# Masked attention: one exponential of 1024 columns over two score banks instead of two of 512

## What is computed

```
scores = jnp.einsum('bgrqd,bgkd->bgrqk', q, k) / jnp.sqrt(jnp.float32(HD))
scores = jnp.where(causal_mask[None, None, None, :, :], -jnp.inf, scores)
scores = jnp.where(padding_mask[:, None, None, None, :], -jnp.inf, scores)
w = jax.nn.softmax(scores, axis=-1)
out = jnp.einsum('bgrqk,bgkd->bgrqd', w, v)
```

## Time and profile before

| | us |
|---|---|
| median of three runs | 1663.35 |
| profiled execution, own time | 1665.44 |
| its span | 1663.5 |
| masked attention, end of its last result on DVE | 554 |
| exponentials of this block (L703), busy | 138.5 |

### The profile page before, as it was taken

One profiled execution on the slowest core, in us unless ns is written; L12 is line 12 of the kernel. 1 busy time (PEld: TensorE's weight loads), 2 busy tenths in 40 slices (PEclk: granted clock), 3 DMA queues, 4 the chain that ended last, 5 costly groups with the idle time before them and its releaser, 6 DMA issues. The chain is left out here.

```text
span 1663.5 us, 22309 instructions
## 1 busy us (share of the span) xinstructions
PE 1410.6 (85%) x8402; PEld 662.6 (40%) x8402; DVE 811.4 (49%) x1326; ACT 722.6 (43%) x1356; POOL 401.5 (24%) x475
## 2 busy tenths in 40 slices
PE   4587786786766688988589999997999999999998
PEld 3254453453432244544212222223444444444443
DVE  6564465465463578775376666652640320320220
ACT  2175556455446277777336556564440220220220
POOL 7111011011002367767322222214540000000000
PEclk9598998898988799999879999998999999999999
DMA  5636535525423201011353434323331001000000
GB/s 151 140 100 167 131 110 160 135 84 145 117 70 108 89 19 33 33 45 50 90 153 111 139 116 138 100 90 114 110 106 64 12 1 45 31 0 25 26 0 26
DMA packets 89283, 140.65 MB, mean 85 GB/s; under 512 B 8264, under 2 KB 47752, under 8 KB 88656
## 3 DMA queue, kind: packets, MB, share of 16 engines
q1 hardware_dynamic: 76384, 114.16, 24.6%
q10 hardware_dynamic: 12800, 25.17, 4.7%
HBM read 105.85 MB, written 33.46 MB: 84 GB/s over the span
## 5 line engine op out<-in xcount | busy, mean ns | idle before, releaser
L1634 DVE TENSOR_REDUCE c_negmax<-c_psA 128x1 f32<-128x512 f32 x256 | 165.7, 682 | 88.9 <-PE c_psA L1699 87.5
L1966 PE MATMUL d_psGU<-d_zt_hi,d_w_hi 128*128 128x512 bf16 x512 | 195.6, 382 | 3.7 <-ACT d_silu L1899 2.3
L830 DVE TENSOR_REDUCE a_negmax<-a_psX 128x4 f32<-128x1024 f32 x128 | 151.0, 1217 | 95.7 <-PE a_psX L1049 95.7
L1966 PE MATMUL d_psGU<-d_zt_lo,d_w_hi 128*128 128x512 bf16 x512 | 195.5, 382 | 0.0
L1966 PE MATMUL d_psGU<-d_zt_hi,d_w_lo 128*128 128x512 bf16 x512 | 195.3, 381 | 0.0
L1899 ACT ACTIVATE d_silu<-d_psGU 128x512 f32<-128x512 f32 x64 | 38.2, 597 | 348.3 <-PE d_psGU L1966 348.3
L1592 ACT ACTIVATE c_probs<-c_psB 128x512 f32<-128x512 f32 x256 | 140.1, 594 | 108.7 <-PE c_psB L1712 108.6
L703 ACT ACTIVATE a_probs<-a_psB 128x512 f32<-128x512 f32 x256 | 138.5, 596 | 98.6 <-PE a_psB L1061 73.7
L1929 DVE TENSOR_TENSOR d_h<-d_psGU,d_silu 128x512 f32<-128x512 f32 x64 | 44.2, 691 | 223.4 <-PE d_psGU L1966 223.1
L1049 PE MATMUL a_psX<-a_ks,a_qs 113*128 113x256 bf16 x512 | 88.6, 312 | 70.4 <-DMA a_qs<-q_scr 46.8
L1061 PE MATMUL a_psB<-a_qs,a_ks 115*128 115x256 bf16 x512 | 94.0, 299 | 40.2 <-ACT a_probs L703 28.6
(11 more groups left out here) (217 smaller groups left out, 2589.9 us busy)
## 6 DMA issues: line engine op xcount, KB each, us to landing
a_tern_stage<-in_w ACTq DMA_DIRECT2D x32, 768.0 KB, 4.7
d_weight_stage<-in_w_last SPq DMA_DIRECT2D x24, 512.0 KB, 3.7
a_ks<-k_scr SPq DMA_DIRECT2D x8, 768.0 KB
a_qs<-q_scr SPq DMA_DIRECT2D x8, 768.0 KB
c_ks<-k_scr SPq DMA_DIRECT2D x48, 128.0 KB, 2.6
c_qs<-q_scr SPq DMA_DIRECT2D x48, 128.0 KB, 3.0
a_xz<-in_x SPq DMA_DIRECT2D x32, 128.0 KB, 7.0
a_ctx<-in_ctx_t SPq DMA_DIRECT2D x8, 512.0 KB, 9.2
```

The costliest lines, as they stand in the source:

```text
L830: v.tensor_reduce(negm[:, u, :], X[:, 2 * (u % 2):2 * (u % 2) + 2, :].rearrange("p a (j k) -> p (a j) k", k=SEQ), AX.X, ALU.max, negate=Tr ...
L1634: v.tensor_reduce(negm[:, u:u + 1], A[:, u % 2, :], AX.X, ALU.max, negate=True)\
L1966: last = pe.matmul(GU[:, 2 * up + i % 2, :], wgu[wh][:, i, up, k, :], zt[zh][:, k, :], start=(k == 0 and j == 0), stop=(k == DC - 1 and j ...
```

## The change

Line numbers in the text are those of the kernel before.

The two exponentials of a pair become one ACTIVATE that reads both banks, 1024 columns, and writes the whole pair of `a_probs`. `score_units` is raised once a pair, by the second unit; `exp_done` once a pair. On PE only the first unit of a pair waits, for the exponential of the pair before it (all of it); the second unit waits for nothing. `weigh` waits for the same exponentials as before, counted in pairs; SyncE's wait at the start of batch 7 is the same point, counted in pairs.

```diff
--- before.py
+++ after.py
@@ -552,7 +552,7 @@
                     stack(b + 2)
                 if b + 1 == BATCH:
 
-                    sp.wait_ge(s["exp_done"], 4 * GROUPS * b)
+                    sp.wait_ge(s["exp_done"], 2 * GROUPS * b)
                     front.sync(sp)
                 for j in range(QJ):
                     sp.wait_ge(s["x_updated"], ST * b + j // (QJ // ST) + 1)
@@ -697,12 +697,10 @@
 
                 g = e // 2
                 need(act, s["pv_done"], GROUPS * b + g - 1)
-                for jj in range(2):
-                    u = 2 * e + jj
-                    act.wait_ge(s["score_units"], 4 * GROUPS * b + u + 1)
-                    act.activation(pr[:, e % 4, :, jj * P:(jj + 1) * P].rearrange("p r (a i) -> p a r i", a=2),
-                                   B[:, u % 2, :].rearrange("p (a r i) -> p a r i", a=2, r=SHARE), ACT.Exp,
-                                   scale=HD ** -0.5).then_inc(s["exp_done"], 1)
+                act.wait_ge(s["score_units"], 2 * GROUPS * b + e + 1)
+                act.activation(pr[:, e % 4].rearrange("p r (a i) -> p a r i", a=QJ),
+                               B[:].rearrange("p j (a r i) -> p (j a) r i", a=2, r=SHARE), ACT.Exp,
+                               scale=HD ** -0.5).then_inc(s["exp_done"], 1)
 
             def attend(b):
                 for g in range(1, GROUPS):
@@ -1052,21 +1050,23 @@
                 last.then_inc(s["max_units"], 1)
 
             def score_unit(b, e, jj):
-                par, grp, kt, u = b % 2, e // 2, e % 2, 2 * e + jj
+                par, grp, kt = b % 2, e // 2, e % 2
                 queries = qflat[par][0:K_ALL, SHARE * grp * SEQ:SHARE * (grp + 1) * SEQ]\
                     .rearrange("p (c j n) -> p c j n", c=2, j=QJ)
-                need(pe, s["exp_done"], 4 * GROUPS * b + u - 1)
+                if jj == 0:
+                    need(pe, s["exp_done"], 2 * GROUPS * b + e)
                 for a in range(2):
                     j = 2 * jj + a
-                    last = pe.matmul(B[:, u % 2, a * SEQ:(a + 1) * SEQ], ks[par][0:K_ALL, j, grp, kt * P:(kt + 1) * P],
+                    last = pe.matmul(B[:, jj, a * SEQ:(a + 1) * SEQ], ks[par][0:K_ALL, j, grp, kt * P:(kt + 1) * P],
                                      queries[:, :, j, :], start=True, stop=True)
-                last.then_inc(s["score_units"], 1)
+                if jj == 1:
+                    last.then_inc(s["score_units"], 1)
 
             def weigh(b, grp):
 
                 par, k = b % 2, GROUPS * b + grp
                 need(pe, s["os_copied"], k)
-                pe.wait_ge(s["exp_done"], 4 * (k + 1))
+                pe.wait_ge(s["exp_done"], 2 * (k + 1))
                 for kt in range(2):
                     for r in range(SHARE):
                         last = pe.matmul(OS[32 * r:32 * r + 32, 0:SEQ], v1[par][:, kt, grp, :],
```

## The result

| | before | after |
|---|---|---|
| median of 8 runs each, us | 1663.13 (1659.86 to 1668.74) | 1672.81 (1668.29 to 1677.24) |
| profiled execution, own time, us | 1665.44 | 1676.21 |
| start of the block's last result on DVE, us | 553.20 | 563.66 |

The ratio is 1.0051, 95% interval 1.0035 to 1.0066: the change costs 8.5 us (5.8 to 11.0). (A cost in this document is the ratio times the median of the kernel before; the two medians lie 9.7 us apart.) It is slower by more than 0.2%, as forecast, and 1672.8 lies in the range of 1668 to 1684. The profiled execution of the changed kernel is 3.4 us above its median; the traces differ by 10.8 us, 10.5 us of it in the masked attention.

A forecast was written before the change was run, and what follows sets the result against it. In groups 4 to 7 PE's instruction list with its waits sets the pace. Losses of 4.7 + 3.7 + 2 x 0.8 + 1.4 + 1.1 = 12.5 us on the 1663.35 us median gave 1676 us, range 1668 to 1684.

The forecast's parts named there:

- Sign and cause: Whole kernel: slower by over 0.2%, chance 0.85, because ACT and PE must wait for each other's whole pair.
- The round trip: Between PE and ACT, neighbouring exponentials start at least 1.78 us apart, 2.22 at the low clock; before 0.96 to 1.30.
- ACT's saving: All 128 pairs: 0.055 us less ACT work each, 7.0 us in all, worth nothing where ACT idles.
- Head: Start of batch 0, with no landing to hide behind: pair 8 starts 3.7 us later, the largest single term.
- it assumes that the clock rises about when it did: Start of batch 0: condition of the 3.7 us; 2.5 if the clock rises sooner, 6 if later.
- Ring: Groups 3 to 7 of batches 0 to 3: each group's loss counted separately, 1.18 us a batch, 4.7 in all.
- group 6 into 7, 0.28: Batch 2: pair 15 starts at 228.37 and `weigh` at 229.01 instead of 228.73, losing 0.28 us.
- Batch 4: Maxima and pairs at the low clock some 15 us after the landing; loses 1.4 us, its first 0.8 hidden.
- Batches 5 and 6: ACT's waits for DVE's ternary rounding absorb the pairs before them; 0.8 us lost in each batch.
- The clock rival: Batches 0 to 6: longer PE pauses drop the clock in a third of 40 groups, about 24 us, 1700; chance 0.08.
- Batch 7: ACT's 4.34 us wait hides the first half; pairs 9, 12 and 15 then lose 0.4, 0.4 and 0.3, 1.1 us.
- The landing waits: PE's waits for the queries in batches 1 to 3, 5 and 6 shorten by about 1 us; vanishing would refute the prediction.

The follow-up runs named there:

- e1: Kernel before, keeping two exponentials of 512 but with both waits of the change (ACT for both units, PE for the whole pair before); 1677.9 us, ratio 1.0084.
- e6: Kernel before, with one exponential of 1024 only for pairs 0 to 6 of batches 1, 2, 3, 5 and 6; 1663.1 us, ratio 0.9993.
- e5: Kernel before, with one exponential of 1024 only for pairs 0 to 7 of batch 0; 1669.4 us, ratio 1.0032.
- e10: The change again, semaphores counted in units and PE's second unit keeping an already met wait; 1676.4 us, ratio 1.0071 to the kernel before.
- e4: The change, but pairs 0 to 7 of batch 0 keep two exponentials of 512; 1672.1 us, ratio 1.0054 to the kernel before.
- e11: e4 unchanged, measured again beside e10 on the same chip; 1671.9 us, ratio 1.0047 to the kernel before.
- e9: Kernel before, with each group's first maximum unit issued ahead of score pair 2g + 2 in groups 3 to 7; 1653.1 us, ratio 0.9932.
- e8: The change, with the first maximum unit ahead of score pair 2g + 2 in groups 3 to 7; 1666.6 us, ratio 1.0009 to the kernel before.
- e12: e8, but halves for pairs 0 to 7 of batch 0 and, in group 6, `weigh` ahead of pair 15; 1656.1 us, 0.9954 to the kernel before.
- e2: Kernel before, two exponentials of 512, only PE waiting for both exponentials of the pair before; 1670.1 us, ratio 1.0049.

## Why the prediction was right

**Sign and cause: right.** The round trip is there to the hundredth (1.78 us in the ring; 2.15 instead of 2.22 at the low clock), the waits alone make the loss (e1), and where the landing wait covers groups 0 to 2 neither the loss nor ACT's saving is seen (e6). The sum was 12.5 us; measured were 8.5 and 11.8. Term by term:

- **ACT's saving, 0 on the path: perhaps too low.** With the waits held equal (e1 against the two measurements of the change) it gives 2 to 5 us by the medians, with intervals that overlap, and 0.8 to 1.5 us in the traces of batches 0 to 3. I had used the 1.02 us in each step, so the sum had it inside; what I called worthless is only the part where ACT idles for another reason.
- **Head, 3.7 us: too small; 4.8 in the trace, 5.3 alone (e5), 4.5 between e10 and e11.** The step that failed was "it assumes that the clock rises about when it did". It rose some 8 us later; the 6 us that I had given as the bound for this hold. Up to pair 4 the delay was as forecast (2.5 us), and the excess of 1.1 us came while the clock was low; no run changes the clock alone, so that it is the cause is argued.
- **Ring, 1.18 us per batch: too large, 0.75.** The steps from group 3 to 6 lost 0.32 + 0.28 + 0.23 (5.06 - 4.74, 4.81 - 4.53, 4.81 - 4.58 between first maxima on DVE), close to the 0.35 + 0.30 + 0.25. The step that failed is "group 6 into 7, 0.28". I added it to the 0.25 of group 5, as if the delay of pair 14 moved exponential 14 too. But exponential 14 starts where ACT's own list lets it: 3.98 us behind pair 13 before (223.31, 227.29) and 3.97 after (228.83, 232.80). From pair 13 to `weigh` of group 6 it was 5.42 us before (223.31, 228.73) and 5.57 after (228.83, 234.40), so both steps together lost 0.15 where I had added 0.25 and 0.28: the two delays start from the same pair 13, and the larger of them counts, not the sum. The last step went from 4.44 to 4.36 us.
- **Batch 4, 1.4 us: 2.4 in the trace. Batches 5 and 6, 0.8 each: 0.25 and 1.3 from the landing on, and 1.6 and 2.9 in e10.** These three scatter: e4 and e11, with the same exponentials there, have 1.3 and 0.0 us in batch 4, -0.1 and -0.4 in batch 5, 3.0 and 1.2 in batch 6. For batch 4 I had also read the clock wrongly. I put its low clock at some 15 us after the landing (321.91), but there it was high at first (1.00 from 323 to 327 us, 0.50 from 328 to 337) and 0.68 over the 15 us. In batch 6 of the change and of e10 the clock fell behind the longer pause (0.57 and about 0.6 where it had been 1.00). The clock rival, as written, did not come (24 us in a third of 40 groups; batches 0 to 6 have only 35 from group 3 on, which makes 21 us); a small piece of it did, in the head and in batch 6.
- **Batch 7, 1.1 us: nothing seen** (59.54 against 59.40 us). Batch 7 takes between 56.5 and 62.3 us over the kernels, so this stays untested.

The landing waits of batches 1 to 3, 5 and 6 did not vanish: 6.1 to 6.4 us, where they had been 6.5 to 8.0, 0.9 us less on average where I had said about 1. DVE's last result came at 563.66 where I had said near 566. The Trainium skill (Perfetto Trace Analysis, section Matmuls) advises rotation through banks, and its rule held: the price in this kernel is 8.5 to 11.8 us for 128 pairs. Two more banks, with which whole pairs could rotate, are not there (all eight are in use), and I haven't tried another division.

Open: the scatter of the landings and of the first maximum behind them, and with it the 4 us of e9 that I can't place. A hint is that in batches 1 to 3 the three kernels with the maximum unit first (e8, e9, e12) average 5.5 us from the landing to group 3's first maximum and the eleven others 5.9; single values lie between 4.8 and 6.6. Open too are how much the clock alone costs, and why e2 costs 8 us when batch 0 (+2.4) and the ring (+0.56 in each of batches 1 to 3) make 4.1. Its profiled execution is one of its fastest, at +2.2.

## What to carry to other kernels

Merging two instructions that each free half of a buffer also merges their signals: before counting the overhead saved, write out the round trip between the two engines (here 1.02 + 0.06 + 0.70 us against 0.96 to 1.30) and look where nothing else fills it. Where a group of instructions waits in an in-order list, ask what independent work stands behind it; moving one such unit ahead brought 11 us here (some 7 of it placed in the trace), more than the 7.8 us of ACT's work that merging the exponentials saved. And where two delays start from the same event and meet at one engine, take the larger, not the sum.

## What was not expected of the hardware

- PE's clock went with the pauses ahead of a stretch, so a pause may cost more than its length. In the head, with pauses of 1.1 us in every 2.15 the clock stayed at the 1.2 GHz level 8 us longer (0.51 against 0.98 from 88 to 96 us; 0.50 or 0.51 in all five kernels with both waits there, 0.83 and 0.86 with one, 0.91 to 1.00 with none), and the head passed the forecast by 1.1 us. In batch 6 a pause of 2.47 us instead of 1.73 was followed by four microseconds at 0.57. The fourteen traces agree on this place: in the five with both waits there and the maximum unit in its old place (the change, e10, e1, e4, e11) PE paused 2.47 to 2.53 us and 0.57 to 0.61 followed, in the nine others 0.94 to 2.24 us and 1.00 followed.
- An ACTIVATE that reads 1024 columns over two PSUM banks takes 1021 ns. The copy of 1024 columns (1024 ns) crosses a bank too, so the line that I drew through it doesn't test this; but the two that stay in one bank, 385 ns for 256 columns and 596 for 512, lead to 385 + 3 x 211 = 1018 ns. Crossing the bank costs nothing that can be seen.
- The same stretch of instructions repeats to 0.01 us between batches 1 to 3 (the ring, 23.35 or 24.11 us), and mostly to 0.05 us between kernels with the same waits there (24.10 to 24.16, once 24.19), where no weight piece lands late. The time from the projections to a landing varies by 4 us. A trace's totals can't be compared to a microsecond here; its segments between landings can.
